# Attention pass of a graph network kernel: four instead of three of sixteen tiles get their P rows by TensorE look-ups, block marks made once a turn

## What is computed

```python
def _L3_gnn_ref(x, node_anchor, attn_w, attn_b, edge_anchor, edge_w, edge_b, edge_index):
    ...
    w = jax.nn.softmax(x @ attn_w.T + attn_b, axis=1)
    xp = x + w @ node_anchor
    src, dst = (edge_index[0], edge_index[1])
    combined = jnp.concatenate([x[src], x[dst]], axis=1)
    b = jax.nn.softmax(jax.nn.leaky_relu(combined @ edge_w.T + edge_b, 0.01), axis=1)
    ep = b @ edge_anchor
    agg = jnp.zeros_like(xp).at[src].add(ep).at[dst].add(ep)
    return xp + 0.5 * agg
```

## Time and profile before

| | |
|---|---|
| median of 3 runs | 5394.46 us |
| profiled execution, its own time | 5397.56 us |
| its span in the trace | 5395.8 us |
| TensorE matmul busy | 3268.4 us, 61% |
| TensorE weight load busy | 2184.8 us, 40% |
| VectorE busy | 2027.4 us, 38% |
| ScalarE busy | 957.3 us, 18% |
| GpSimd busy | 3073.1 us, 57% |

### The profile page before, as it was taken

One profiled execution on the slowest core, in us unless ns is written; L12 is line 12 of the kernel. 1 busy time (PEld: TensorE's weight loads), 2 busy tenths in 40 slices (PEclk: granted clock), 3 DMA queues, 4 the chain that ended last, 5 costly groups with the idle time before them and its releaser, 6 DMA issues. The chain is left out here.

```text
span 5395.8 us, 69161 instructions
## 1 busy us (share of the span) xinstructions
PE 3268.4 (61%) x19534; PEld 2184.8 (40%) x19535; DVE 2027.4 (38%) x6104; ACT 957.3 (18%) x2127; POOL 3073.1 (57%) x3180
## 2 busy tenths in 40 slices
PE   4357544557997645555554444444479956777777
PEld 2124322233444334333433333333334435666665
DVE  7441101014114322222222222222231157888886
ACT  0010000001002200000000000000010016888885
POOL 5777777730000477777776777777700006777773
PEclk8678767778998755555555555555589976888887
DMA  8521010132223422222222111111132202323222
GB/s 224 142 96 49 24 48 24 48 64 104 95 95 107 143 72 76 80 80 80 76 80 60 53 53 53 53 53 53 53 122 95 95 24 57 67 68 69 66 67 64
DMA packets 370426, 408.73 MB, mean 76 GB/s; under 512 B 89191, under 2 KB 305078, under 8 KB 360374
## 3 DMA queue, kind: packets, MB, share of 16 engines
q1 hardware_dynamic: 268854, 295.73, 17.3%
q0 software_dynamic: 101504, 112.13, 8.8%
HBM read 299.65 MB, written 107.98 MB: 76 GB/s over the span
## 5 line engine op out<-in xcount | busy, mean ns | idle before, releaser
L633 POOL DMA_INDIRECT GS<-xw_table,stage x1664 | 1572.4, 945 | 1208.0 <-issue 1159.5
L1120 PE MATMUL psum<-HA,HT 128*128 128x512 fp8e4 (+1 forms) x5733 | 1213.1, 374 | 483.9 <-DMA HA<-adj 437.2
L1072 PE MATMUL psum<-GS 128*128 128x96 f32 x3328 | 774.4, 409 | 1034.7 <-DMA GS<-xw_table,stage 1021.7
L1072 PEld LDWEIGHTS psum<-GS 128*128 128x128 f32 x3328 | 697.8, 310 | 1110.6 <-issue 1110.6
L633 POOL DMA_INDIRECT HA<-p_table,stage x676 | 652.3, 965 | 750.3 <-ACT stage L916 550.1
L667 POOL DMA_INDIRECT adj<-cell_value,cell_i x832 | 841.5, 1011 | 290.5 <-issue 249.3
L1120 PEld LDWEIGHTS psum<-HA,HT 128*128 128x128 bf16 x5733 | 550.3, 100 | 1120.9 <-issue 484.9
L1577 DVE TENSOR_TENSOR HA<-HA,psum 128x96 f32 x208 | 53.0, 255 | 1355.4 <-PE psum L1072 1355.4
L1563 DVE TENSOR_SCALAR GS<-iota,HT,wt 128x96 f32<-128x96 f32 x1680 | 436.6, 355 | 158.5 <-issue 157.5
L1831 DVE SCALAR_TENSOR_TENSOR GS<-psum,keep,O 128x512 f32<-128x512 f32 (+1 forms) x26 | 18.7, 719 | 1081.9 <-PE psum L1140 764.7
L731 ACT ACTIVATE stage<-cell_i 128x16 int32 (+1 forms) x104 | 22.2, 215 | 1265.9 <-PE psum L1072 1265.9
(11 more groups left out here) (340 smaller groups left out, 3619.9 us busy)
## 6 DMA issues: line engine op xcount, KB each, us to landing
HA<-adj SPq DMA_DIRECT2D x39, 1600.0 KB, 6.5
HA<-adj SPq DMA_DIRECT2D x39, 1536.0 KB, 9.8
HT<-dst_rows SPq DMA_DIRECT2D x212, 256.0 KB
xw_table<-HT SPq DMA_DIRECT2D x100, 512.0 KB, 3.2
adj<-O SPq DMA_DIRECT2D x13, 3136.0 KB, 26.9
GS<-xw_table,stage POOLq DMA_INDIRECT x1664, 2.5
adj<-cell_value,cell_i POOLq DMA_INDIRECT x832
HA<-p_table,stage POOLq DMA_INDIRECT x676
```

Of the source, the lines that this page charges most:

```text
L633: nc.gpsimd.indirect_dma_start(out=to, out_offset=None, in_=table, in_offset=bass.IndirectOffsetOnAxis(ap=idx, axis=0)).then_inc(done, 16)
L1072: last = nc.tensor.matmul(bank[h][:, 0:WINDOW], G3[g][:, j, :], S_pair[h][:, t, :], start=(t == 0), stop=(t == 2 * GT - 1))
L1120: last = nc.tensor.matmul(bank[s][:, 0:w], Hs4[:, b, t, :], adj_tile[s][:, b * GW:b * GW + w], start=(b == 0 and t == 0), stop=(b == SRCS ...
```

## The change

`LOOKED` goes from 3 to 4: twelve gathers a turn instead of thirteen, four transposes, twelve look-up matmuls, a copy of 4 x 128 columns, two products of two tiles each, and a sum over four tiles. The block marks of the looked tiles are no longer made by themselves. Instead `block_columns` makes the marks of all 16 tiles of the next turn, in the place where it made those of the present one, and there are two buffers for them; `take_sources` reads the first four tiles of it, `by_block_and_anchor` reads the buffer filled a turn earlier. Before the loop, `block_columns(0, 0)` takes the place of `source_blocks(0)`. Buffers move to other places in SBUF; the rest is unchanged.

```diff
--- before.py
+++ after.py
@@ -26,7 +26,7 @@
 PAIRS = GROUPS // 2
 WINDOW = 96
 LAG = 5
-LOOKED = 3
+LOOKED = 4
 SAGE1_STEPS = 8 * 13 + 1
 SAGE_STEPS = SAGE1_STEPS + 6 * 13
 TRASH_COL = 6300
@@ -221,7 +221,7 @@
         M_l3 = O[:, 0:L16 * 245].rearrange("p (j m) -> p j m", m=245)
         lo_l3 = [t.rearrange("p (j d) -> p j d", d=P) for t in (O[:, 3920:3920 + L16 * P], A[:, 2048:2048 + L16 * P])]
         oht_l3 = A[:, 0:2048].bitcast(BF).rearrange("p (g h e) -> p g h e", g=4, h=2)
-        hi_l3 = A[:, 4096:4096 + L16 * 49].rearrange("p (j d) -> p j d", d=49)
+        hi_l3 = [t.rearrange("p (j d) -> p j d", d=49) for t in (A[:, 4096:4096 + L16 * 49], GS[:, 0:L16 * 49])]
         Qp = A[:, 4880:4880 + NB * B5 // 2].bitcast(BF)
         Qp3 = Qp.rearrange("p (b a) -> p b a", a=B5)
         Q = A[:, 5260:5260 + NB * A5]
@@ -233,11 +233,10 @@
         r5 = A[:, 6136:6136 + L16]
         b5p = A[:, 6152:6152 + L16 * B5 // 2].bitcast(BF).rearrange("p (j a) -> p j a", a=B5)
         products_p = tail[:, 1152:1152 + LOOKED * 245].rearrange("p (j a d) -> p j a d", d=49, a=A5)
-        Pp = tail[:, 1888:1888 + NB * B5 // 2].bitcast(BF)
+        Pp = tail[:, 2132:2132 + NB * B5 // 2].bitcast(BF)
         Pp_part = [Pp[:, t * NB * A5:(t + 1) * NB * A5] for t in range(PARTS)]
-        src_rows = tail[:, 2264:2264 + LOOKED * P // 2].bitcast(BF)
-        hi_p = tail[:, 2456:2456 + LOOKED * 49].rearrange("p (j d) -> p j d", d=49)
-        iota_b = tail[:, 2604:2604 + P].bitcast(BF)
+        src_rows = tail[:, 2508:2508 + LOOKED * P // 2].bitcast(BF)
+        iota_b = GS[:, 2 * GT * P:2 * GT * P + P].bitcast(BF)
         n5 = [T[:, 5300 + i * NB * A5:5300 + (i + 1) * NB * A5].rearrange("p (b a) -> p b a", a=A5) for i in range(3)]
         zeros = Wcat[0][:, 0:4 * P]
         anchors = Wcat[1][0:UW, 0:UB * P]
@@ -247,7 +246,7 @@
         bank = [psum[:, i * 512:(i + 1) * 512] for i in range(8)]
         by_dst = psum[:, 0:2 * 512]
         b5 = bank[3][:, 0:L16 * A5].rearrange("p (j a) -> p j a", a=A5)
-        looked_p = [bank[7][:, 0:245], bank[7][:, 245:490], bank[6][:, 0:245]]
+        looked_p = [bank[7 - j // 2][:, j % 2 * 245:(j % 2 + 1) * 245] for j in range(LOOKED)]
         iota49 = bank[3][:, L16 * A5:L16 * A5 + 49]
 
 
@@ -1701,10 +1700,10 @@
                         then(V.tensor_tensor(rest_w[:, :], rest_w[:, :], src_i[:, bass.ds(k * GT, GT)], ALU.add))
                         then(V.tensor_tensor(rest_w[:, :], rest_w[:, :], outside[:, :], ALU.mult))
                         then(V.tensor_scalar(rest_w[:, :], rest_w[:, :], 1.0, None, ALU.subtract))
-                        then(V.tensor_tensor(hi_l3[:, 0:GT, :], iota[:, 0:49].unsqueeze(1).broadcast_to([P, GT, 49]), over(hi4, GT, 49), ALU.is_equal))
+                        then(V.tensor_tensor(hi_l3[0][:, 0:GT, :], iota[:, 0:49].unsqueeze(1).broadcast_to([P, GT, 49]), over(hi4, GT, 49), ALU.is_equal))
                         for j in range(GT):
                             V.tensor_scalar(lo_l3[0][:, j, :], iota[:, 0:P], rest_w[:, j:j + 1], None, ALU.is_equal)
-                            last = V.tensor_tensor(M_l3[:, j, :].rearrange("p (d a) -> p d a", a=A5), over(hi_l3[:, j, :], 49, A5),
+                            last = V.tensor_tensor(M_l3[:, j, :].rearrange("p (d a) -> p d a", a=A5), over(hi_l3[0][:, j, :], 49, A5),
                                                    b5[:, j, :].unsqueeze(1).broadcast_to([P, 49, A5]), ALU.mult)
                         last.then_inc(rest_ready5, 1)
                         with dve.Fori(0, WINDOWS) as w:
@@ -2104,22 +2103,22 @@
             V.memset(anchors, 0.0).then_inc(anchors_clear, 1)
             ch(V.tensor_tensor(X3, X3, H3, ALU.add))
 
-            def source_blocks(it):
-
-                return V.tensor_tensor(hi_p, iota49.unsqueeze(1).broadcast_to([P, LOOKED, 49]),
-                                       over(src_hi[:, bass.ds(it * L16, LOOKED)], LOOKED, 49), ALU.is_equal)
+            def block_columns(it, u):
+
+                return V.tensor_tensor(hi_l3[u], iota49.unsqueeze(1).broadcast_to([P, L16, 49]),
+                                       over(src_hi[:, bass.ds(it * L16, L16)], L16, 49), ALU.is_equal)
 
             def take_sources(it, u):
 
                 dve.wait_ge(p_looked, it + 1)
-                chosen = hi_p.unsqueeze(2).broadcast_to([P, LOOKED, A5, 49])
-                V.tensor_tensor(products_p[:, 0:2], bank[7][:, 0:490].rearrange("p (j a d) -> p j a d", d=49, a=A5), chosen[:, 0:2], ALU.mult)
-                V.tensor_tensor(products_p[:, 2], bank[6][:, 0:245].rearrange("p (a d) -> p a d", a=A5), chosen[:, 2],
-                                ALU.mult).then_inc(p_taken, 1)
+                chosen = hi_l3[u][:, 0:LOOKED, :].unsqueeze(2).broadcast_to([P, LOOKED, A5, 49])
+                for of, looked in ((slice(0, 2), bank[7]), (slice(2, 4), bank[6])):
+                    last = V.tensor_tensor(products_p[:, of], looked[:, 0:490].rearrange("p (j a d) -> p j a d", d=49, a=A5), chosen[:, of], ALU.mult)
+                last.then_inc(p_taken, 1)
                 dve.wait_ge(p_taken, it + 1)
                 return V.reduce_sum(p_rows[u][:, 0:LOOKED, 0:A5], products_p, AX.X)
 
-            ch(source_blocks(0))
+            ch(block_columns(0, 0))
             ch(take_sources(0, 0))
             STEPS = 9
             with dve.Fori(0, ITERS // 2) as i2:
@@ -2148,11 +2147,10 @@
                             V.tensor_scalar(lo_l3[u][:, t, :], iota[:, 0:P], neg_lo[:, bass.ds(it * L16 + t, 1)], 0.0,
                                             ALU.add, ALU.is_equal)
 
-                    def block_columns():
+                    def next_block_columns():
 
                         dve.wait_ge(parts5, it + 1)
-                        V.tensor_tensor(hi_l3, iota49.unsqueeze(1).broadcast_to([P, L16, 49]),
-                                        over(src_hi[:, bass.ds(it * L16, L16)], L16, 49), ALU.is_equal)
+                        block_columns(it + 1, 1 - u)
 
                     def by_block_and_anchor(g):
 
@@ -2160,7 +2158,7 @@
                         dve.wait_ge(scattered, it * 4 + g + 1)
                         at = slice(g * GT, (g + 1) * GT)
                         V.tensor_tensor(M_l3[:, at, :].rearrange("p j (d a) -> p j d a", a=A5),
-                                        hi_l3[:, at, :].unsqueeze(3).broadcast_to([P, GT, 49, A5]),
+                                        hi_l3[u][:, at, :].unsqueeze(3).broadcast_to([P, GT, 49, A5]),
                                         b5[:, at, :].unsqueeze(2).broadcast_to([P, GT, 49, A5]), ALU.mult).then_inc(ready5, 1)
 
                     dve.wait_ge(gathered16[u], 16 * (L16 - LOOKED) * (i2 + 1))
@@ -2171,10 +2169,9 @@
                     source_rows(3)
                     dve.wait_ge(logits_done, it + 3)
 
-                    then(V.scalar_tensor_tensor(z5, z5, 0.01, z5, ALU.mult, ALU.max), block_columns)
+                    then(V.scalar_tensor_tensor(z5, z5, 0.01, z5, ALU.mult, ALU.max), next_block_columns)
                     then(V.reduce_max(m5, z5, AX.X))
                     V.tensor_tensor(z5, z5, over(m5, L16, A5), ALU.subtract).then_inc(soft_in, 1)
-                    source_blocks(it + 1)
                     for g in range(3):
                         columns(g)
                     dve.wait_ge(soft_exp, it + 2)
```

## The result

The changed kernel takes 5433.13 us, the median of four runs (5430.96 to 5436.13), against 5395.86 for the kernel before (four runs as well, one more than in the table ahead): 1.007 of it, 95% interval 1.0058 to 1.0082. The profiled execution took 5434.0 us with a span of 5432.2, 36.4 us more than the span of before.

What follows compares the result with a forecast made beforehand. TensorE's row of work was taken as the bound, each of 51 turns growing to one clock cycle of 17.07 us: +36.7, +1.4 ahead of the loop, +0.9 in the last turn, +39.0 in all, 5433 us, range 5408 to 5440.

Steps and rivals of the forecast that it cites:

- What bounds the kernel: Attention pass: TensorE's fixed row of work sets the turn; VectorE has 1.7 us to spare, GpSimd's queue runs ahead.
- What is removed: One gather a turn, 1.26 us of GpSimd, gives back at most 7 us; small block marks, 0.30 us of VectorE, go.
- The natural turn: TensorE's turn in the kernel before: three long clock cycles of 17.07 us and one short of 13.65, giving 16.21 us.
- the first two rivals: First: short low stretches stay, 5411 us, 12%. Second: TensorE's growth covered, GpSimd the bound, 5386 (6%) or 5330 us (3%).
- VectorE and ScalarE: Wider product and sum, +0.26 us each, net +0.2 to +0.3 a turn, hidden in VectorE's spare time; ScalarE's copy +0.13.
- TensorE: Three more matmuls, net +0.30 us a turn, and one more transpose, +0.11: together +0.41, between 0.30 and 0.78.
- What the turn becomes: Added TensorE work pushes out the short low stretches, so every turn takes one whole clock cycle, 17.07 us.
- The distance from fall to look-ups: Time from the clock's fall to the second look-ups settles near 1.3 us, where the low stretch is always long.
- The lower border: From about 0.15 us of added TensorE work (distance 0.7 us), every turn takes one clock cycle.
- The upper border: Up to about 0.95 us of added TensorE work (distance 2.5 us), the turn stays one clock cycle.
- The third rival: Low stretch beyond 6.8 us, or VectorE's product on TensorE's path, past 0.95 us added: 17.5 us a turn, 5455 us, 5%.
- The sum: Loop +36.7 us, ahead of it +1.4, last turn +0.9: in all +39.0, 5433 us against the median.

Runs made afterwards that it cites:

- b_look2: Kernel before, with the logit look-ups of groups three and four made twice with the same values: 5435.33 us, 1.0071.
- a_no3mm: Changed kernel without the three added look-up matmuls, the fourth transpose and wider copy and products kept: 5398.78 us, 1.0003.
- b_marks: Changed kernel with three tiles looked up and thirteen gathers as before, only the block marks made a turn ahead in two buffers: 5394.90 us, 0.9999.
- a_pool13: Changed kernel with the thirteenth gather put back, into a buffer nobody reads: 5436.69 us, 1.0072.
- b_at: Kernel before, with four block numbers loaded between the scatter by source and the scatter by destination instead of ahead of the second look-ups: 5397.36 us, 0.9999.
- both changes: Kernel before, with four block numbers loaded behind the scatter by source and ScalarE's order changed: 5396.73 us, 0.9998.
- a_look2: Changed kernel with the look-ups of the third and fourth group made twice: 5439.34 us, 1.0079.
- a_look5: Changed kernel with the look-ups of the third and fourth group made four times each: 5437.88 us, 1.0074.
- a_noT: Changed kernel without the fourth transpose, ScalarE copying three tiles, the twelve look-up matmuls kept: 5434.31 us, 1.0074.
- a_act: Changed kernel with ScalarE's order alone changed, second group's marks ahead of the exponents and the copy ahead of the source distances: 5433.23 us, 1.0068.

## Why the prediction was right

- **What bounds the kernel.** TensorE's row of work, VectorE and GpSimd with time to spare: for the changed kernel this is shown from three sides. Work added on TensorE alone gives the whole loss (b_look2), taking only TensorE's three matmuls out takes it away (a_no3mm), and neither the marks (b_marks) nor the gather (a_pool13) moves the time. For the kernel before it is half of the truth. VectorE had time to spare, but GpSimd had almost none: with TensorE's row shortened (b_at, both changes) its gathers hold the turn at 16.31 us, beside 16.35 in the kernel before and TensorE's own 16.29 (a_no3mm). The small wait for gathered rows (10.9 us) told rightly that a lighter GpSimd gains nothing there; it did not tell that the next bound was 0.1 us away.
- **What is removed.** The gathered-row waits of 10.9 us did vanish and gave nothing, since TensorE's turn stood above them. The natural turn that the prediction took from four turns, 16.21 us, was a little low: without those waits it is 16.29 (a_no3mm), with 39 low stretches of 6.8 us and 11 of 3.4, so not quite one in four. The forecast doesn't hang on it, the first two rivals do (by some 4 us).
- **VectorE and ScalarE.** The sum was forecast at 0.921 + 0.26 = 1.18 us and took 1.176; the copy at 0.60 and took 0.574. The product (0.658) never waited in the loop (idle 0.0 at L2116).
- **TensorE.** Three matmuls at the low clock: 2.42 - 1.80 = 0.62 us against 0.60. The transpose was the term that was mis-sized: 0.11 us in the sum, 0.00 measured. The traces show why: the register instructions begin at 4896.2 us, while the transposes run from 4896.28 to 4896.92, and from transposes to look-ups it is 3.62 us with three and with four. The Trainium skill's page "TensorE: Matmul & The Clock Gate" (Part 2, step-by-step), which the prediction set against the row, says that the sequencer takes the next instruction without waiting for the array to drain; with that the traces agree. It did not change the forecast, as the prediction said, because 0.30 already lay above the border.
- **What the turn becomes.** Forecast 17.07, measured 17.04 over all turns and 17.07 once settled (the first two were 16.07 and 16.77). The distance from fall to look-ups: forecast "near 1.3", measured 1.0 and 1.3 in neighbouring turns (falls at 4898.85 and 4915.9, look-ups at 4899.90 and 4917.24). Every kernel that lost (the changed one, b_look2, a_look2, a_look5, a_noT, a_pool13, a_act) has settled turns of 17.07 us, whatever its added work. The lower border, 0.15 us of added work, holds as far as it was tried: the transpose alone (0.0) fell below it, the three matmuls (0.3) lay above. The upper border, 0.95 us, was wrong: the prediction had only followed cycles of 10.2 us high and 6.8 low, and at 1.2 us more than the change's own work the pattern turned into one with 13.65 high and 3.4 low and the same total (a_look5). The third rival, 5455 us, rested on that border; at 1.5 us of added work the turn was 17.09 us, not 17.5.
- **The sum.** Loop +35.1 (forecast +36.7), after the last logit sum 63.1 against 62.1, +1.0 (+0.9). Ahead of the loop the first logit sum came 29.0 us after the first gather (4471.07) instead of 27.3 (4472.47): +1.7 (+1.4). The passes before happened to be 1.4 us shorter in this execution, so +36.4 in the traces; forecast +39.0. In the medians it is 5433.1 - 5395.9 = +37.3 us. That the forecast median (5433) met the measured one to the microsecond is partly luck: single terms were off by 1 to 2 us, and the median of the kernel before rose from 5394.5 to 5395.9 with its fourth run.

The border that the prediction took from two turns (0.55 us ahead of the look-ups short, 0.6 long) can be read more closely in the traces of before, b_marks and a_no3mm, whose TensorE rows take the same time. In the settled turns, every low stretch of 3.4 us began 0.32 to 0.57 us ahead of the second look-ups, and every one of 6.8 us 0.57 us or more. What is not settled is why it lies there, and why the high stretches of a_look5 are longer: no run varied either by itself.

## What to carry to other kernels

Ask of a loop with an idle gap on TensorE not only how long its work is but how its turn stands to the pattern of the granted clock: close below a whole cycle, 0.3 us of added work cost 0.7 us a turn here, and 1.2 us more cost next to nothing. Before moving work onto an engine to relieve another, read whose wait ends last: the change lost 37 us until TensorE's gap and ScalarE's order were mended, and gained 67 to 69 after. And measure how close the next engine stands, since without the change the same two repairs gained nothing. Look where an engine's program loads registers: behind 3.4 us of queued matmuls the loads cost nothing here, ahead of the look-ups seven numbers left 3.0 us of idle time, most of it for what follows each number and not for the loads.

## What the runs showed that was not expected

- A settled turn of 17.07 us holds over a wide span of work, by two shapes of the clock's pattern: 10.2 us high and 6.8 low with 0.3 to 0.7 us of added work, 13.65 high and 3.4 low with 1.5 (a_look5, granted clock 0.723 over the span against 0.706).
- Loads of four block numbers behind 3.4 us of queued matmuls cost 0.0 us; ahead of the look-ups the gap had been 3.1 us, and ScalarE's marks came 2.1 us into it.
- 48 more matmuls of 15 columns a turn (1.2 us) cost the changed kernel 5 us in the medians (5437.9 against 5433.1), while three more of 245 columns (0.62 us at the low clock) make the 34 us between a_no3mm and the changed kernel: the length of an addition did not tell its price.
- The kernel before had two bounds within 0.1 us a turn, TensorE's row (16.29 us) and GpSimd's gathers (16.31), of which its waits showed only the first.
